# Expert weights over the query and key tiles of a two-layer perceiver kernel

## What is computed

```
x = x + L0_xattn(layernorm(x), ctx)        # 8 heads of 64
x = x + L0_attn(layernorm(x))              # causal, 16 heads of 16
x = x + L0_ffn(layernorm(x))
x = x + L1_xattn(layernorm(x), ctx, ctx)   # 16 heads of 16
x = x + L1_attn(layernorm(x))              # linear attention and an MLP of 1024
x = x + L1_ffn(layernorm(x))

def L0_ffn(x):   # 16 experts (256 -> 352 -> 256), the best 2 of each token, 20 slots each
    ...
    expert_outputs = vmap(mlp)(expert_inputs, w_gate, w_up, w_down)   # silu(h @ wg) * (h @ wu) @ wd
    return x + mlp(x, sw_gate, sw_up, sw_down) + output_tokens        # one shared expert

def L1_ffn(x):   # 8 experts (256 -> 1024 -> 256), each takes its 32 best tokens
    G, idx = top_k(softmax(x @ Wr).T, 32)
    h = gelu(einsum('ekd,edh->ekh', x[idx], W1) + b1)
    X_e = einsum('ekh,ehd->ekd', h, W2) + b2
    return zeros.at[idx].add(G[..., None] * X_e)
```

## Time and profile before

| | |
|---|---|
| median of three runs | 1229.85 us |
| the profiled execution | 1231.95 us |
| its span, first to last instruction | 1230.0 us |
| TensorE busy | 1178.4 us, 96% |
| VectorE, ScalarE, GpSimd busy | 54%, 55%, 17% |
| mean granted TensorE clock | 0.979 of full speed |
| HBM read, written | 124.87 MB, 38.67 MB |
| share of the chain that ended last: TensorE, VectorE, DMA | 89%, 7%, 2% |

### The profile page before, as it was taken

One profiled execution on the slowest core, in us unless ns is written; L12 is line 12 of the kernel. 1 busy time (PEld: TensorE's weight loads), 2 busy tenths in 40 slices (PEclk: granted clock), 3 DMA queues, 4 the chain that ended last, 5 costly groups with the idle time before them and its releaser, 6 DMA issues.

```text
span 1230.0 us, 29349 instructions
## 1 busy us (share of the span) xinstructions
PE 1178.4 (96%) x10142; PEld 945.5 (77%) x10142; DVE 670.0 (54%) x1138; ACT 671.0 (55%) x1092; POOL 213.1 (17%) x312
## 2 busy tenths in 40 slices
PE   6999999999999999999777899999999999999998
PEld 5887777777777777777665688888887888888784
DVE  5999444443444343434753588888885444444442
ACT  2897333333333333333120388788886899988420
POOL 0000100000000000000003377778750110000110
PEclk8999999999999999999979999999998999999989
DMA  3444700010011001000336267667665895555442
GB/s 132 137 138 119 312 26 26 26 34 26 26 27 33 26 26 34 26 26 26 116 116 278 92 225 230 223 221 235 222 219 176 289 303 198 185 184 181 158 168 91
DMA packets 62027, 163.97 MB, mean 133 GB/s; under 512 B 6640, under 2 KB 7088, under 8 KB 56304
## 3 DMA queue, kind: packets, MB, share of 16 engines
q1 hardware_dynamic: 53360, 118.54, 29.4%
q0 software_dynamic: 8640, 45.05, 10.2%
HBM read 124.87 MB, written 38.67 MB: 133 GB/s over the span
## 4 chain that ended last, share of the span: by engine, by line
PE 89%; DVE 7%; DMA 2%; ACT 1%; issue 1%; POOL 0%; DVEq 0%; ACTq 0%
PE ps L657 61%; PE ps L908 8%; PE ps L846 8%; PE ps L645 2%; PE ps L699 2%; DMA ring<-ex_in 2%; PE ps L710 1%; PE ps L714 1%; PE ps L711 1%; PE ps L713 1%; PE ps L712 1%; PE ps L1210 1%; PE ps L1044 0%; PE ps L1066 0%; PE ps L1186 0%
## 5 line engine op out<-in xcount | busy, mean ns | idle before, releaser
L1427 DVE TENSOR_TENSOR wide<-wide,probs 128x1024 f32<-128x1024 f32 x97 | 118.9, 1225 | 264.5 <-ACT probs L504 264.5
L1359 DVE TENSOR_TENSOR wide<-ps,wide 128x512 f32<-128x512 f32 (+1 forms) x196 | 187.1, 954 | 32.7 <-PE ps L657 28.0
L515 ACT ACTIVATE probs<-ps 128x1024 f32<-128x1024 f32 x196 | 190.2, 1023 | 22.5 <-PE ps L657 22.3
L504 ACT ACTIVATE probs<-ps 128x512 f32<-128x512 f32 x196 | 117.2, 598 | 113.0 <-PE ps L657 112.9
L489 ACT CAST wide<-ps 128x512 bf16<-128x512 f32 x294 | 162.4, 587 | 29.9 <-PE ps L657 25.3
L657 PE MATMUL ps<-q_ha,t_ha 128*128 128x512 f32 x392 | 156.9, 400 | 3.8 <-DVE q_le L1287 3.8
L496 ACT COPY v_sb<-ps 128x512 f32<-128x512 f32 x98 | 57.6, 588 | 178.5 <-PE ps L657 178.5
L1364 DVE TENSOR_TENSOR wide<-wide 128x512 bf16<-128x512 bf16 (+1 forms) x196 | 108.6, 554 | 13.4 <-ACT wide L489 3.3
L846 PEld LDWEIGHTS ps<-probs,v_sb 128*64 128x64 f32 x1568 | 83.6, 136 | 34.4 <-ACT probs L504 34.0
L657 PE MATMUL ps<-q_ab,q_hk 128*128 128x512 f32 x392 | 108.0, 397 | 0.0
L846 PE MATMUL ps<-probs,v_sb 128*64 128x128 f32 x1568 | 107.0, 279 | 0.0
(11 more groups left out here) (374 smaller groups left out, 2235.1 us busy)
## 6 DMA issues: line engine op xcount, KB each, us to landing
raw<-ctx_in SPq DMA_DIRECT2D x147, 256.0 KB, 2.6
k_mem<-q_hk SPq DMA_DIRECT2D x49, 512.0 KB, 3.0
v_mem<-probs SPq DMA_DIRECT2D x49, 256.0 KB, 3.5
wide<-v_mem SPq DMA_DIRECT2D x49, 256.0 KB, 4.3
ring<-ex_in POOLq DMA_DIRECT2D x8, 1152.0 KB, 12.4
q_le<-k_mem SPq DMA_DIRECT2D x17, 512.0 KB, 4.4
q_ab<-k_mem SPq DMA_DIRECT2D x16, 512.0 KB, 4.4
q_hk<-k_mem SPq DMA_DIRECT2D x16, 512.0 KB, 4.5
```

Of the source, the lines that this page charges most:

```text
L504: act.activation(probs[:, j * 2048 + u * 512:j * 2048 + (u + 1) * 512], ps[:, s_bank[u], :], ACT.Exp).then_inc(sem("exp0"), 1)
L515: act.activation(probs[:, at:at + 1024], ps[:, bank:bank + 2, :].rearrange("p b n -> p (b n)"), ACT.Exp).then_inc(sem("exp1"), 1)
L1359: dve.tensor_tensor(r, ps[:, b:b + half // 512, :].rearrange("p b n -> p (b n)"), r, ALU.max)\
L1427: dve.tensor_tensor(run[:, 0:1024], run[:, 0:1024], e, ALU.add).then_inc(sem("lsum"), 1)
```

## The change

Over the four query and key tiles a fifth one, `weights_q`, of 8192 floats per partition is laid at the same addresses. In layer 0 it gives three more places (9, 10, 11), for experts 9, 10 and 11, loaded behind the last product of the first cross attention (`pv0`), under one semaphore. There are twelve places now, expert e goes to e modulo 12, so only 12 to 16 are second tenants: 12 waits for `down_s`, 13 to 16 for `down0` 1. In layer 1 experts 4 and 5 lie in it whole and are loaded behind `x_done` 4 like 2 and 3. `keep_warm(20, 4)` ahead of `up0(2)` goes, `keep_warm(26, 2)` ahead of `up0(3)` becomes `keep_warm(20, 2)`, `up1(1)` moves ahead of `turn1(0)`, and `keep_warm(12, 3)` ahead of `down1(1)` goes. VectorE's five memsets move from behind `keep_out0(1)` to behind `keep_out0(2)`.

```diff
-        q_ha = sb("q_ha", [P, 2048], F32R)
-        q_ab = sb("q_ab", [P, 2048], F32R)
-        q_hk = sb("q_hk", [P, 2048], F32R)
-        q_le = sb("q_le", [P, 2048], F32R)
+        with ExitStack() as shared:
+            q_ha, q_ab, q_hk, q_le = (shared.enter_context(nc.sbuf_tensor(name, [P, 2048], F32R))
+                                      for name in ("q_ha", "q_ab", "q_hk", "q_le"))
+        weights_q = sb("weights_q", [P, 8192])
...
-                   pieces((wlb[:, LBW - 2048:LBW], 2)) + pieces((ring, 4))[2:],
-                   pieces((wx1[:, 2048:3072], 1)) + pieces((ring[:, W1:2 * W1], 4))[1:],
+                   pieces((weights_q[:, 0:W1], 4)), pieces((weights_q[:, W1:2 * W1], 4)),
...
-            wa[:, 0:W0], wa[:, W0:2 * W0], probs[:, 0:W0], wide[:, 0:W0], wlb[:, 0:W0]]
-        place0 = [(e % len(places), e // len(places) + 1) for e in range(E0)] + [(len(places) - 1, 2)]
+            wa[:, 0:W0], wa[:, W0:2 * W0], probs[:, 0:W0], wide[:, 0:W0], wlb[:, 0:W0]] + [
+            weights_q[:, i * W0:(i + 1) * W0] for i in range(3)]
+        place0 = [(e % len(places), e // len(places) + 1) for e in range(E0 + 1)]
...
+            pool.wait_ge(sem("pv0"), 2 * TILES)
+            for e in range(9, 12):
+                load0(e)
             pool.wait_ge(sem("x_done"), 1)
...
             pool.wait_ge(sem("down_s"), 1)
-            load0(9)
+            load0(12)
             pool.wait_ge(sem("down0"), 1)
-            for e in range(10, 14):
-                load0(e)
-            pool.wait_ge(sem("down0"), 2)
-            for e in range(14, E0 + 1):
+            for e in range(13, E0 + 1):
                 load0(e)
             pool.wait_ge(sem("split0"), GROUPS)
-            pool.wait_ge(sem("pv0"), 2 * TILES)
             groups(pool, split_all)
...
             pool.wait_ge(sem("x_done"), 4)
-            load1(2)
-            load1(3)
-            load1(5, range(1))
+            for e in range(2, 6):
+                load1(e)
             load1(6, range(2))
             pool.wait_ge(sem("y"), 4)
             load1(6, range(2, 4))
             pool.wait_ge(sem("y"), 5)
             load1(7)
-            pool.wait_ge(sem("x_done"), 5)
-            load1(4, range(2))
-            pool.wait_ge(sem("up1"), 2)
-            load1(5, range(1, 2))
-            pool.wait_ge(sem("down1"), 1)
-            load1(4, range(2, 4))
-            load1(5, range(2, 4))
...
             down0(1)
-            keep_warm(20, 4)
             up0(2)
             spread0(1)
             turn0(2)
             down0(2)
-            keep_warm(26, 2)
+            keep_warm(20, 2)
             up0(3)
...
             up1(0)
+            up1(1)
             turn1(0)
             down1(0)
-            up1(1)
             turn1(1)
             spread1(0)
-            keep_warm(12, 3)
             down1(1)
...
+            clear_maxima(1, (0,))
+            hidden0(2)
+            turned0(2)
+            keep_out0(2)
             for q in (q_la, q_b):
                 dve.memset(q[CB:P, 0:512].bitcast(F32), 0.0)
                 dve.memset(q[0:CB, 512:1024].bitcast(F32), 0.0)
             link(dve.memset(q_le[96:P, :].bitcast(F32), 1.0))
-            clear_maxima(1, (0,))
-            hidden0(2)
-            turned0(2)
-            keep_out0(2)
             hidden0(3)
```

More of the change, by code:

```diff
@@ L178, in perceiver, with place_sem @@
         out0 = [probs[:, W0 + 1536:W0 + 1792], yb[:]]
-        def w_sem(e, part):
-            return (f"w{part + 1}_{e}", 32) if e in (4, 5) else (f"w_{e}", 64)
+        def place_sem(e):
+            place, loads = place0[e]
+            return ("place_q", 48) if place >= 9 else (f"place{place}", 16 * loads)
         rest = ring[:, 2 * W1:4 * W0]
@@ L378, in load0 @@
             def load0(e):
-                place = place0[e][0]
-                pool.dma_start(places[place], ex0_in[e]).then_inc(sem(f"place{place}"), 16)
+                pool.dma_start(places[place0[e][0]], ex0_in[e]).then_inc(sem(place_sem(e)[0]), 16)
             one = ones[:, 0:1].to_broadcast([P, GK])
@@ L433, in load1 @@
                     pool.dma_start(expert1[e][i], ex1_in[e, :, i * 1024:(i + 1) * 1024])\
-                        .then_inc(sem(w_sem(e, i // 2)[0]), 16)
+                        .then_inc(sem(f"w_{e}"), 16)
             pool.dma_start(b1, b1_in).then_inc(sem("b1_loaded"), 16)
@@ L1006, in weights0 @@
             def weights0(e):
-                place, loads = place0[e]
-                pe.wait_ge(sem(f"place{place}"), 16 * loads)
-                return places[place]
+                pe.wait_ge(sem(place_sem(e)[0]), place_sem(e)[1])
+                return places[place0[e][0]]
             w = weights0(0)
@@ L1184, in up1 @@
                             if half == 0 and k == 0:
-                                pe.wait_ge(sem(w_sem(e, 0)[0]), w_sem(e, 0)[1])
+                                pe.wait_ge(sem(f"w_{e}"), 64)
                             last = pe.matmul(ps[32 * c:32 * c + 32, 2 * b + half, :], qt[:, k * D + e * TOPK:k * D + (e + 1) * TOPK],
@@ L1207, in down1 @@
                     for c in range(4):
-                        if m == 0:
-                            pe.wait_ge(sem(w_sem(4 * b + c, 1)[0]), w_sem(4 * b + c, 1)[1])
                         last = pe.matmul(ps[32 * c:32 * c + 32, bank, 0:D],
```

## The result

The changed kernel takes 1216.84 us (median of 4 runs, 1215.71 to 1217.41), the kernel before on the same chip 1229.69 us (4 runs, 1228.57 to 1231.4). The ratio is 0.9896, 95% interval 0.9879 to 0.9914: faster by 1.0%, with an interval that leaves out 1. The profiled execution of the change took 1215.71 us (span 1213.8).

A forecast was written before the change was run, and what follows sets the result against it. TensorE, busy 96% of the span, bounds the kernel; only its waits for weights and filler can go. -6.41 - 1.38 - 4.95 = -12.74 us from 1231.95 gives 1219.2, less 2.1 to the median: 1217.1 us, range 1214.5 to 1222.0.

The forecast's parts named there:

- Batch 2 starts at batch 1's end, -6.41: First layer's feed-forward: with experts 9 to 12 there early, batch 2 starts at 656.59 instead of 663.00, -6.41 us.
- the shorter filler, -1.38: First layer, ahead of batch 3: filler cut from 26 calls to 20, 12 instructions fewer, -1.38 us.
- Expert 16 in time: First layer: the burst's fourth expert lands at 665.5, 2.4 us ahead of batch 3's start; loss taken as 0.
- VectorE's memsets, 0: First layer: the five moved memsets end by 668.8, ahead of batch 3's VectorE product at 670.7; cost 0.
- POOL's splits, 0 of 0 to +1.0: First layer: POOL's context splits run earlier, beside VectorE's steps of batches 1 and 2; bounds 0 and +1.0 us, 0 taken.
- Second layer, -4.95: Second layer's feed-forward: experts 4 and 5 early, `up1(1)` directly behind `up1(0)`; `down1(1)` starts at 1217.60, not 1222.55, -4.95 us.
- The 0.5 us allowed for the turn-around: Second layer, between the two down products: expected gap 1.45 us, with 0.5 us allowed either way.
- The median: Whole kernel: the profiled execution lay 2.1 us above the median, so 1219.2 us became 1217.1 us.
- Rival 1, small losses: Clock fall (+1.7), late landing (+0.7) and splits (+1.0) eat part of the gain: 1219.5 to 1222 us; chance 0.16.
- Rival 2: One gain fails, say first layer's batch 3 gets its weights only at 674.5: 1223.7 us; chance 0.05.
- Rival 3, starved for instructions: Full DMA queue at loop exit and second-layer burst delays instruction fetches: 1237 us, chance 0.04; just eating the gain, 0.03.
- Rival 4: The change doesn't do what it says: `weights_q` lies elsewhere than over the four tiles; same times, no chance given.

The follow-up runs named there:

- Experiment 4: The change with the first layer's fillers as before (20 calls ahead of `up0(2)`, 26 ahead of `up0(3)`): 1222.52 us, ratio 0.9944.
- experiment 6: The change, but POOL starts its splits for layer 1 only behind batch 2 (`down0` 3): one execution, 1213.82 us.
- Experiment 7: The change, but expert 12 is loaded at the head of the burst with 13 to 16, a burst of five: one execution, 1218.39 us.
- experiment 5: The change without any filler ahead of `up0(3)` (`keep_warm(20, 2)` taken out): one execution, 1214.14 us.
- experiment 2: The kernel before with only the second layer's part of the change; first layer as before: 1224.88 us, ratio 0.9966.
- experiment 8: The change, but experts 9 to 11 are loaded behind experts 4 and 5 and the wait for `k_diag`: one execution, 1216.11 us.
- experiment 1: The kernel before with only the first layer's part of the change; second layer as before: 1219.46 us, ratio 0.9921.
- experiment 9: The change with 12 instead of 20 filler calls ahead of batch 3 and the second layer's up and down products woven in halves: 1215.03 us, ratio 0.988.
- experiment 12: The kernel of experiment 9, unedited, run again beside a version with nine filler calls in the query-rests gap: 1216.13 us, ratio 0.9888.
- woven kernel: The change with 12 instead of 20 filler calls ahead of batch 3 and the second layer's products interleaved in halves: 1215.03 us, again 1216.13 us.
- experiment 10: The change itself, unedited, run on the same chip as the kernel of experiment 9: 1215.62 us, ratio 0.9887.

## Why the prediction was right

Forecast 1217.1 us, range 1214.5 to 1222.0; measured 1216.84. By its steps:

- *Batch 2 starts at batch 1's end, -6.41, and the shorter filler, -1.38.* The sum, -7.79, came out at -7.87. Experiment 4 shows that the filler carries most of it: with the weights early and the filler kept, 6.13 of it are gone. The prediction counted the removed filler inside the stretch and did not say that the edit of the fillers was the larger part. Both are needed: the weights make the cut of the filler ahead of batch 2 possible.
- *Expert 16 in time.* Margin forecast 2.4 us, measured 1.7: the landing took 14.0 us instead of 13.4. The prediction took 13.4 because the slot in the burst was the same, and priced the earlier splits for VectorE alone; what they changed is a context load that now falls into the burst (experiment 6). The 2.6 to 3 us that it read for each expert are also too even: the third of the burst landed 4.2 us behind the second, before. Experiment 7, with the landing at 16.2, shows the price when it is late: 1.38 us, of which 1.31 is the wait.
- *VectorE's memsets, 0.* They ended at 667.05 and the product of batch 3 came at 669.81, 2.76 us later (forecast 668.8 and 670.7, 1.9 apart). Hidden, and in experiment 5 with 1.16 us between them still.
- *POOL's splits, 0 of 0 to +1.0.* Right for VectorE by experiment 6: 13.13 us beside them, 13.14 without. The Trainium skill's rule (SBUF — State Buffer, section Who interferes with whom) has a condition, two inputs in SBUF or a two-port mode, and these steps with an input in PSUM don't meet it; the trace agrees, 0.56 us each in both. Where the condition is met, at VectorE's products of query rests, the trace of before shows no wait for a whole instruction but both engines slower side by side: the last two of the four products took 1.00 and 1.01 us instead of 0.68, and the three splits there 1.00 to 1.06 instead of 0.60.
- *Second layer, -4.95.* -4.95 against the profile that the prediction was made from; the forecast for the start of `down1(1)`, 13.49 behind `up1(0)`, held to 0.01 us in eight profiles (the change twice, experiments 2 and 4 to 8). The 0.5 us allowed for the turn-around was not needed. But what was taken away, the wait, differs between executions: 3.59 against experiment 1's second layer. The size was that of one profile. The count of the loads was wrong, without harm: the burst behind `x_done` 4 grew from 11 pieces (9 and 2) to 18, not from 13, so by seven pieces and not by five. The last of the 18 landed at 1170.03 and the last of expert 7 at 1182.38, 10 us ahead of `up1(0)` at 1192.80.
- *The median.* The prediction moved its sum from the profiled execution to the median by subtracting 2.1, and the difference of medians, 12.85, is that of the sum, 12.74. Since both waits of before were shorter in other profiles (the first layer's stretch by 1.15 in experiment 2, the second's by 1.36 in experiment 1), up to 2.5 us of the 12.85 may be something else; what, no run shows. So the mechanism is shown, and that the forecast came within 0.3 us is in part luck.
- *Rival 1, small losses.* Not seen: the clock was 1.00 over 640 to 690 of the change without the fillers. Its price for a fall, 1.7 us, is above what the fall at the start of layer 1's cross attention cost up to the next product of scores (0.75 to 1.4 us). *Rival 2* was 1.7 us of margin away. *Rival 3, starved for instructions*: nothing in the loop exit with 415 GB/s beside it (experiment 8); and around its second place, the burst in the second layer, it took 52.38 us from the copy of `xt` behind pass 2 to `up1(0)`, before and after alike. The Trainium skill's rule on a taken branch out of the fetched window (Runtime: NRT & Kernel Launch, section Instruction fetch mechanics) may hold, but no run here shows a stall by it. *Rival 4*: the records name `weights_q` as an input of `up0(2)`, which doesn't tell where it lies. That it lies over the four tiles is read from the code, which gives them back before it takes `weights_q`; the times can't tell.

## What to carry to other kernels

Memory that is dead in a stage is worth what TensorE waits for the reload of reused buffers; read that as the distance between the end of the earlier product and the start of the waiting one, filler included, and cut the filler in the same edit, since with the weights in time it is the greater part of the loss. A gap between two products is not idle time until the other work of that engine in it is counted: here it was transposes. A step that one engine does sooner can release another engine's transfer into a burst (experiment 6). And when a step comes sooner, look at the next place where TensorE stands still, 2.45 us here: a gap that did no harm in one version can cost its clock in the next, and filler may help in such a gap, not where a product could run.

## What the runs showed of the hardware

- **The same gap, with and without a fall of the clock.** TensorE's wait for VectorE's query rests lasted 2.45 to 2.47 us in each of the 13 profiles without filler in it. In 5 of them (before, experiments 5, 7, 9 and 12) the clock fell to 0.50 at its end or within 1 us behind it, in 8 it stayed at 1.00. In the one profile with 2.17 us of filler in it, it stayed at 1.00. The woven kernel had the fall in both of its profiles, the change in neither of its two. From the copy of `xt` to the first product of scores it took 9.55 to 9.57 us without the fall, and 10.3 to 11.0 with it. What in the earlier work decides it stays open.
- **A fall that comes and goes in one kernel.** In the second pass of layer 1, the first profile of the change and then the second, unedited:

```profile
924.00:926.00 2.00, 1.15 (x5) 0.93 (x4) 0.00 (x0) 2.00 (x3) 0.00 (x0) 0.50 0.00 0
```

```profile
924.00:926.00 2.00, 1.32 (x28) 1.19 (x32) 0.00 (x0) 2.00 (x3) 0.00 (x0) 1.00 0.00 0
```

  From the maxima ahead of it (`DVE sm`, 914.42 and 914.09) to the copy of `xt` behind the pass (1140.42 and 1138.19) it took 226.00 us with the fall and 224.10 without: 1.9 us of spread between executions that no edit of these kernels touched. Of the 14 profiles, the stretch took 224.10 us in four (experiments 5, 6, 9 and 10) and 225.95 to 226.34 in the other ten.
- **Landings vary by more than a microsecond between executions of unchanged code**: 7.8 and 6.5 us for the slowest of the same five loads in the second layer, and for the third of the burst in the first layer 9.8 us in experiment 2 and 11.2 to 11.7 in the other profiles. A margin of 1 us on a landing is not safe, and a wait for one is not a constant. Not all of it is chance: the 0.6 us of the fourth go with the context load beside it.
